# Attention of a fused transformer block: head pairs in the search for the maximum, three score banks, mask and shift through TensorE, loop written out

## The reference, cut to what matters

```
x = x + 0.5 * ffn(layernorm(x))          # x: 2 x 2048 x 256, ffn: 256 -> 1024 -> 256, then 5 spike steps
x = x + attn(layernorm(x))
x = x + 0.5 * ffn(layernorm(x))

def attn(x):                             # 16 heads of 16, causal
    q, k = rope(x Wq'), rope(x Wk'); v = x Wv' + bv
    scores = q k' / 4, future keys masked out
    return softmax(scores) v  Wo' + bo
```

## Time and profile before

| | us |
|---|---|
| median of 3 runs | 1601.37 (1593.75 to 1605.08) |
| the profiled execution: its time | 1608.4 |
| the profiled execution: its span | 1606.7 |
| mean granted clock of TensorE | 0.904 |
| busy in the span: PE / PEld / DVE / ACT / POOL | 1381.6 / 821.8 / 1139.5 / 860.6 / 229.9 |

### The profile page before, as it was taken

How to read it: one execution, slowest core, us unless ns; L and a number is a source line. 1 busy time by engine, 2 the same in 40 slices (tenths; PEclk the granted TensorE clock), 3 DMA queues, 4 the chain that set the end, 5 groups by cost and what they waited for, 6 DMA issues and landing times. The chain is left out here.

```text
span 1606.7 us, 27137 instructions
## 1 busy us (share of the span) xinstructions
PE 1381.6 (86%) x8384; PEld 821.8 (51%) x8384; DVE 1139.5 (71%) x2689; ACT 860.6 (54%) x1155; POOL 229.9 (14%) x206
## 2 busy tenths in 40 slices
PE   5988888750799999999999989999999976899997
PEld 5877777640443343343343333433433422799986
DVE  5666676821788888877887887888888930567675
ACT  5644444310036666655665665666666655466564
POOL 0012222346001011010010110110110101110100
PEclk9999999875568899997997999999999978899999
DMA  5113333437152062070080260440620002222312
GB/s 204 40 40 105 105 118 100 150 123 95 13 69 34 6 83 24 5 101 8 9 98 5 30 82 5 55 52 6 72 34 5 8 8 68 92 80 92 95 51 66
DMA packets 101898, 97.86 MB, mean 61 GB/s; under 512 B 46288, under 2 KB 85200, under 8 KB 100048
## 3 DMA queue, kind: packets, MB, share of 16 engines
q1 hardware_dynamic: 101744, 95.98, 29.0%
HBM read 57.15 MB, written 37.75 MB: 59 GB/s over the span
## 5 line engine op out<-in xcount | busy, mean ns | idle before, releaser
L1001 ACT ACTIVATE probs<-s_ps 128x1024 f32<-128x1024 f32 (+3 forms) x640 | 542.7, 895 | 327.7 <-PE s_ps L1133 326.4
L1112 PE MATMUL m_ps<-kT,qT 64*128 64x512 f32 (+3 forms) x1280 | 478.9, 478 | 112.9 <-DMA qT<-qkT_parts 55.9
L1026 DVE TENSOR_REDUCE maxes<-m_ps 128x1 f32<-128x512 f32 x768 | 490.8, 684 | 48.5 <-PE m_ps L1112 44.2
L1112 PEld LDWEIGHTS m_ps<-kT,qT 64*128 64x128 f32 x1280 | 217.2, 201 | 502.2 <-DVE maxes L1026 274.0
L1133 PE MATMUL s_ps<-qT,kT 64*128 64x512 f32 (+3 forms) x1280 | 327.3, 416 | 13.8 <-DMA qT<-shiftT 10.5
L1031 DVE CUSTOM_DVE_ANT_0 masked<-m_ps,mask_b 128x384 f32<-128x384 f32 (+3 forms) x512 | 238.3, 488 | 130.6 <-PE m_ps L1112 125.0
L1150 PE MATMUL o_ps<-probs,v_w 128*32 128x512 f32 (+3 forms) x2560 | 322.4, 578 | 0.2 <-POOL probs L974 0.2
L974 POOL TENSOR_SCALAR_AFFINE_SELECT probs<-probs 128x512 f32<-128x512 f32 x128 | 81.6, 637 | 851.8 <-ACT probs L1001 851.8
L1133 PEld LDWEIGHTS s_ps<-qT,kT 64*128 64x128 f32 x1280 | 164.2, 198 | 41.0 <-ACT probs L1001 25.0
L313 ACT ACTIVATE relu_a<-ups_a 128x512 f32<-128x512 f32 x64 | 38.1, 596 | 100.8 <-PE ups_a L562 99.9
L1150 PEld LDWEIGHTS o_ps<-probs,v_w 128*32 128x32 f32 x2560 | 51.9, 111 | 76.5 <-issue 58.9
(11 more groups left out here) (124 smaller groups left out, 1917.7 us busy)
## 6 DMA issues: line engine op xcount, KB each, us to landing
kT<-qkT_parts SPq DMA_DIRECT2D x48, 256.0 KB
qT<-qkT_parts SPq DMA_DIRECT2D x96, 128.0 KB
qkT_parts<-qk_hi_a SPq DMA_DIRECT2D x32, 256.0 KB, 3.0
qkT_parts<-qk_lo_a SPq DMA_DIRECT2D x32, 256.0 KB, 3.4
qT<-shiftT SPq DMA_DIRECT2D x512, 1.0 KB
xin_a<-in_x SPq DMA_DIRECT2D x8, 512.0 KB, 4.0
xres_a<-in_x SPq DMA_DIRECT2D x8, 512.0 KB, 4.9
x<-xsum_a SPq DMA_DIRECT2D x8, 512.0 KB, 3.2
```

Of the source, the lines that this page charges most:

```text
L1001: act.activation(probs[:, b % PBUF, 2 * hp:2 * hp + 2, off:CH], s_ps[hp][:, :, off:CH], ACT.Exp, scale=D ** -0.5)\
L1026: dve.tensor_reduce(out, m_ps[:, bank, 0:width], AX.X, ALU.max).then_inc(max_read, 1)
L1112: pe.matmul(m_ps[:, bank, 0:width], qT[of % 2][r0:r0 + HR, j, h // 2, t * P:(t + 1) * P], kT[of % 2][r0:r0 + HR, h // 2, k * CH:k * CH + w ...
```

## The change

What it does: (1) a unit of the maximum is a pair of heads, two matmuls into two banks at once; there are 80 units a group, the ring has two places of two banks, and DVE reduces both heads by one `tensor_reduce` (up to 2 x 512). (2) On the diagonal PE adds the mask by two more matmuls (bf16, identity times mask, 128 x 128), and the `tensor_tensor_reduce` goes. (3) The scores have three banks instead of four, one head each, in turn; ACT takes the exponential head by head (1280 instructions instead of 640), and PE waits for each bank by itself. (4) The two parts of the shift are turned by a transpose on PE, as an item of the ring three units behind the last unit of the step; DVE copies the 32 rows out of PSUM, and SP writes them by 4 DMAs. (5) The loop is written out; loads of the next group are spread over six slots. (6) In a slot PE's order is: scores of `hp` 0, first item, scores of `hp` 1, second item, products, the other items.

```diff
-        HR, MB = P // 2, 3
+        SB, MB = 3, 2
+        HR = P // 2
-        s_ps = [pb(f"s_ps{p}", [P, 2, CH]) for p in range(2)]
-        m_ps = pb("m_ps", [P, MB, CH])
+        s_ps = pb("s_ps", [P, SB, CH])
+        m_ps = pb("m_ps", [P, MB, 2, CH])
...
-        UNITS = [(j, t, 2 * hp + par, k, CH if k < j else P * (t + 1))
-                 for j in range(NJ) for t in range(T) for hp in range(G // 2) for k in range(j + 1) for par in range(2)]
+        UNITS = [(j, t, hp, k, CH if k < j else P * (t + 1))
+                 for j in range(NJ) for t in range(T) for hp in range(G // 2) for k in range(j + 1)]
-            cost = [u[4] + 110 for u in UNITS]
+            cost = [2 * u[4] + 110 for u in UNITS]
...
+            for n in range(GROUPS):
+                for j in range(NJ):
+                    last = max(i for i, (_, e) in enumerate(order) if e[0] == "unit" and e[1] == n and UNITS[e[2]][0] == j)
+                    after = [i for i, (_, e) in enumerate(order) if i > last and e[0] == "unit"][:3]
+                    at = after[-1] if after else last
+                    order.insert(at + 1, (order[at][0], ("shift", n, j)))
...
+                        row, c0 = HR * par + KR + a, G * T * a + G * T // 2 * par
+                        out = qT[n % 2][row:row + 1, j, :, :].rearrange("o h (t q) -> o (h t) q", t=T)
+                        sp.dma_start(out.bitcast(F32), shiftT[c0:c0 + G * T // 2, :]).then_inc(shift_in, 16)
...
+                    for h in range(G):
+                        u = G * blk + h
+                        act.wait_ge(s_done, u + 1)
+                        act.activation(probs[:, b % PBUF, h, off:CH], s_ps[:, u % SB, off:CH], ACT.Exp, scale=D ** -0.5)\
                            .then_inc(exp_done, 1)
...
+            def unit(e):                                   # DVE
+                j, t, hp, k, width = UNITS[e[2]]
+                i = ITEM[e]
+                dve.wait_ge(max_done, i + 1)
+                dve.tensor_reduce(maxes[:, j % 2, :, hp, t, k], m_ps[:, i % MB, :, 0:width], AX.X, ALU.max).then_inc(max_read, 1)
...
+            def unit(e):                                   # PE
...
+                free_bank(i)                               # wait: max_read of item i - MB
+                for par in range(2):
+                    r0 = HR * par
+                    mm = pe.matmul(m_ps[:, i % MB, par, 0:width], qT[n % 2][r0:r0 + HR, j, hp, t * P:(t + 1) * P],
+                                   kT[n % 2][r0:r0 + HR, hp, k * CH:k * CH + width], start=True, stop=True)
+                if k == j:
+                    for par in range(2):
+                        mm = pe.matmul(m_ps[:, i % MB, par, t * P:(t + 1) * P], identb[:, :], maskb[:, :],
+                                       start=False, stop=True, skip_group_check=True)
+                mm.then_inc(max_done, 1)
+
+            def turn_shift(e):
+                i = ITEM[e]
+                free_bank(i)
+                pe.wait_ge(neg_step, 3 * step_no(e[1], e[2]) + 3)
+                pe.transpose(m_ps[0:2 * G * T, i % MB, 0, 0:P], negparts[:, :, :].rearrange("p a c -> p (a c)"), ident[:, :])\
                   .then_inc(max_done, 1)
...
+                for par in range(2):                       # scores(n, j, b, hp)
+                    u = G * block_no(n, j, b) + 2 * hp + par
+                    wait(pe, exp_done, u - SB + 1)
+                    r0 = HR * par
+                    pe.matmul(s_ps[:, u % SB, off:CH], kT[n % 2][r0:r0 + HR, hp, b * P:(b + 1) * P],
+                              qT[n % 2][r0:r0 + HR, j, hp, off:CH], start=True, stop=True).then_inc(s_done, 1)
...
+            for g, (n, j, b) in enumerate(slots):
+                items = ITEMS.get(g, [])
+                scores(n, j, b, 0)
+                ring(items[:1])
+                scores(n, j, b, 1)
+                ring(items[1:2])
+                if g >= 2:
+                    products(*slots[g - 2])
+                ring(items[2:])
```

More of the change, by code:

```diff
@@ L764, in place_units @@
             return slots
[L766 to L796, removed]
+        def ring_order():
+            unit_slots, order = place_units(), []
+            for g in range(MAX_FROM, BLOCKS * GROUPS):
+                for n in range(GROUPS):
+                    order += [(g, ("unit", n, u)) for u in unit_slots.get(g - BLOCKS * n, [])]
+                order += [(g, ("sums", n, j)) for n in range(GROUPS) for j in range(NJ) if block_no(n, j + 1, SUM) == g
+                          or j == NJ - 1 and block_no(n + 1, 0, SUM) == g]
+            order.append((BLOCKS * GROUPS, ("sums", GROUPS - 1, NJ - 1)))
+            for n in range(GROUPS):
+                for j in range(NJ):
[3 more added lines that the diff above has]
+                    order.insert(at + 1, (order[at][0], ("shift", n, j)))
+            return order
@@ L798, in wait @@
+        ORDER = ring_order()
+        ITEM = {e: i for i, (_, e) in enumerate(ORDER)}
+        ITEMS = {}
+        for g, e in ORDER:
+            ITEMS.setdefault(g, []).append(e)
+        LAST_UNIT = {(e[1], UNITS[e[2]][0]): e for _, e in ORDER if e[0] == "unit"}
+        TERMS = [(m, x) for m in range(NT) for x in range(2)]
+        LOADS, SHIFTS = 16 * NT * (2 + G) + 32, 16 * 4
         def wait(eng, sem, value):
-            if not isinstance(value, int) or value > 0:
+            if value > 0:
@@ L800, in wait @@
                 eng.wait_ge(sem, value)
[L802 to L837, removed]
@@ L896, in shift @@
+                if m == 0 and x == 1:
+                    sp.dma_start(v_in[p][:, :, :], io["v"][tok:tok + S, group * G * D:(group + 1) * G * D]
+                                 .rearrange("(k p) n -> p k n", p=P)).then_inc(vs_in[p], 16)
+            def shift(n, j):
+                sp.wait_ge(max_read, ITEM["shift", n, j] + 1)
                 for a in range(2):
                     for par in range(2):
-                        row = HR * par + KR + a
-                        out = qT[dn % 2][row:row + 1, j, :, :].rearrange("o h (t r n) -> o (h t) r n", t=T, r=P // VW)
@@ new lines, in store, with moves @@
+            def store(n, j):
+                tok, group = place(n)
+                sp.wait_ge(max_read, ITEM["sums", n, j] + 1)
+                sp.dma_start(io["attn"][tok + j * CH:tok + (j + 1) * CH, group * G * D:(group + 1) * G * D]
+                             .rearrange("(t p) n -> p t n", p=P), att[:, :, :]).then_inc(att_out, 16)
+            def moves(g):
+                for what, n, j in ITEMS.get(g, []):
+                    if what == "shift":
+                        shift(n, j)
+                    elif what == "sums":
+                        store(n, j)
@@ L1010, in _ @@
+                before = (n, j)
+            read_sum(*before)
         @block.vector
         def _(dve):
[L1012 to L1033 removed]
@@ L1184, in _, with ring @@
-            pe.wait_ge(const_in, 32)
-            for x in range(MAX_FROM, 0):
-                for u in unit_slots[x]:
-                    find(0, 0, x, 0, u)
-            steps(pe, body)
+            def ring(items):
+                for e in items:
+                    if e[0] == "unit":
+                        unit(e)
+                    elif e[0] == "shift":
+                        turn_shift(e)
+                    else:
+                        turn_sums(e)
+            pe.wait_ge(mask_ok, 2)
@@ new lines, in _ @@
+            for g in range(MAX_FROM, 0):
+                ring(ITEMS.get(g, []))
+            slots = [(n, j, b) for n, j in steps() for b in range(T * j + T)]
+            for g, (n, j, b) in enumerate(slots):
[7 more added lines that the diff above has]
+                ring(items[2:])
+            for slot in slots[-2:]:
+                products(*slot)
```

369 lines of the change are left out of this document (129 added, 240 removed).

## The result

| | before | after |
|---|---|---|
| median, us | 1603.22 (1593.75 to 1606.89) | 1682.05 (1665.12 to 1688.48) |
| ratio, 95% interval | | 1.048 (1.040 to 1.056) |
| profiled execution: its time | 1608.4 | 1665.12 |
| mean granted clock | 0.904 | 0.926 |
| busy PE / DVE / ACT | 1381.6 / 1139.5 / 860.6 | 1407.4 / 1107.4 / 903.7 |

The change makes the kernel slower by 4.8%. The median moved by 79 us, the two profiled executions by 57: the one of after is its fastest, and the one of before (1608.4) lies above all four runs of its median. DVE has less to do, the clock is higher, and still it takes longer: PE's busy time grew by 26 us, and the rest is waiting.

A forecast was written before the change was run, and what follows sets the result against it. DVE and the banks it frees bound full slots; afterwards a PE-ACT chain would. At 119.4 us a group against 112.1, the main part adds 55 and the last slots 0.5 to 1608.4, about 1664; against the median 1657, range 1610 to 1720.

The forecast's parts named there:

- The chain in each slot: Main part: PE's fourth score waits for ACT's first exponential of the same slot; 2.69 us a full slot, 97.0 a group.
- ACT is not the bound, by-head exponentials cost nothing: Each full slot: four exponentials of 512 take some 2.0 us on ACT, below the chain's 2.69.
- DVE: Main part: a wide reduce takes 1.2 us, so DVE needs 88 us a group against 93 busy before.
- The mask: Diagonal units: PE's mask matmuls cost 0.4 us for each of 19 units not first in their slot, 7.6 a group.
- The clock: Main part: one full slot a group at the low clock, 4.3 us instead of 2.69, adds 1.6 us a group.
- The rest of a group: Per group: chain 97.0, unhidden pairs of item matmuls 8.4, turned sums 2.4 and turned shifts 2.4 us.
- The last 20 slots: End of the attention, without units: 14 full slots and two narrow sets take 49.5 us against 49 before.
- The turned shift: Four a group: PE waits for a reduce and three DVE operations, 0.6 us each, 2.4 a group.
- The old stall of 7.24 us: End of the kernel: scores waited for the shift's 16 DMAs; with four, taking 2.7 us, this stall goes.
- Rival 1: Main part: the chain is there but the rest hides; 106 us a group, 1555 in all; chance 0.22.
- Rival 2: Main part: the clock falls in each slot's gaps, eight more low-clock slots a group; +96 us, 1750; chance 0.12.
- Rival 3: Main part: DVE stays the bound, wide reduce 1.28 us, PE's chain fits beside it; no change, 1600; chance 0.08.

The follow-up runs named there:

- e2: Two score banks instead of three in the changed kernel; 1796.46 us, ratio 1.117 to before.
- e6: Against e3, the products cut into two halves of the queries, one behind each pair of scores; 1563.99 us, ratio 0.971 to before.
- e5: Changed kernel with whole products between the third and fourth score and the second item behind the fourth; 1670.3 us, ratio 1.031 to before.
- e8: Kernel before, each exponential of a pair made as two of one head, banks as they were; 1607.43 us, ratio 0.999 to before.
- e4: Changed kernel without the two mask matmuls of each diagonal unit; 1640.78 us, ratio 1.018 to before.
- e7: e6 without the mask matmuls; 1518.67 us, ratio 0.943 to before.
- e3: Changed kernel with the next group's loads back in pairs at slots 0, 4 and 12; 1633.11 us, ratio 1.017 to before.
- e1: Changed kernel with the whole products moved between the two pairs of scores; 1687.73 us, ratio 1.047 to before.

## Why the prediction was right, and where it wasn't

The forecast was 1657 us, slower; 1682 was measured, within its own range. (By the bounds that it names, half of -12 to +13 us a group makes 1612 to 1706; its 1720 isn't in them.) The median moved by 79 us, where 56 were forecast. By the profiled executions, on which the sum was made, it was 1664 against 1665. That is closer than the steps deserve: it sets an execution of before that is slower than all four of its median against the fastest of after, and the attention itself grew by 63 us where 55.5 were summed, which the shorter untouched parts hid.

- *The chain in each slot*: right, and shown. The full slot without units was priced at 2.69 us and takes 2.67, with two units it was to take 2.8 to 3.0 and takes 2.90. The waits turned from DVE to ACT as the prediction asked (277 us). e2 lengthened the loop by one bank fewer and e6 shortened its stretch, each slot without units to within 0.01 us of what the sum says; e5 was 0.08 shorter than its sum, by the trip.
- *ACT is not the bound, by-head exponentials cost nothing*: right, by e8.
- *DVE*: right. The wide reduce was taken at 1.2 us and has 1.225; 88 us a group were predicted, and 664.5 / 7.5 = 88.6 are there.
- *The mask*: the term was too big. 0.4 us for a unit was 0.27 to 0.31 (e4, e7), so of 7.6 us a group 5.1 to 5.9 were due. I had counted a stand ahead of the mask and part of one behind it, and the second was there without it.
- *The loads*: the step that was missing. The prediction names the part of the change that spreads them over six slots nowhere in its sum, though they stand in the same queue as the attention's store. They cost 7 us in each group that has the stall (e3), 38 us of the main part or 5.1 a group over its 7.5, and 49 us of the median. That is some 60% of the 79 by which the change is slower.
- *The clock*: 1.6 us a group were added for a low clock of unnamed place. With the loads mended the main part runs at 0.99 for 0.96, so some three quarters of its low clock came with the stall of the store. The term stood for something real, but was too small and had no cause.
- The rest of a group: 114.35 us in e3 less the mask's 5.1 to 5.9 is 108.5 to 109.2; the prediction has 97.0 + 8.4 + 2.4 + 2.4 = 110.2. The sum holds to 1 or 2 us; its single terms weren't measured.
- *The last 20 slots*: predicted 49.5, measured 57. The full slots were right. The narrow ones weren't: I took products as narrow as the slot's scores, but the products belong to the slot two earlier. Timeline of after, PE:

```profile
1350.45 0.27 PE L1007 MATMUL m_ps<-ident_b,negparts 128*32 128x128 f32 x1 [1.09 <-DVE negparts L938]
...
1353.59 0.62 PE L1026 MATMUL s_ps<-qT,kT 64*128 64x384 f32 x3
1355.04 1.06 PE L1041 MATMUL o_ps<-probs,v_w 128*32 128x512 f32 x8
1356.04 0.50 PE L1026 MATMUL s_ps<-qT,kT 64*128 64x256 f32 x3
```

The slot of 384 takes 2.45 us (1353.59 to 1356.04) where 2.24 were counted, since products of 512 stand in it; the three narrow slots end at 1360.04, so take 6.45 for 5.43. The turned shift adds a wait of 1.09 (0.6 taken), and from 1363 a stretch at the low clock follows. The old stall of 7.24 us did go: four DMAs take 2.7 us.

So errors of opposite sign met, and that is luck: per group about 2 us too much for the mask and 1 too much in the rest, against 3.5 too little for the stall (5.1 less the 1.6). The 119.4 of the sum and the 119.6 measured (897 / 7.5) agree by that. Rival 1 (the rest hides) is refuted: even with the loads mended the group takes 114.35 us, not 106, and the kernel stays 1.7% slower than before (e3). Rival 2 (the clock falls) is refuted for the change: in its full slots with gaps the clock stays high, 0.96 in the main part and 0.99 in e3. But the last slots of e1, with a gap in each, ran at 0.50 for 60 us, so what it fears does occur, and what starts it isn't shown. Rival 3 (DVE stays the bound) is refuted by its 58 us of waits.

The layout itself is the smaller part of the loss. With the loads in their old places it costs 1.7%, and with the products halved besides it is 2.9% faster than before. That this gain is DVE's smaller load is likely, but no run took the wide reduce alone, and none the written-out loop.

## What to carry to other kernels

Where an engine that works in order feeds a ring of buffers, and a step feeds it once more than it has places (here four scores on three banks), the step is at least the latency of one trip round the ring plus the longest stretch of other work between two feeds, wherever that stretch stands. Splitting it helps (e6), and so does taking something out of it (the item in e5); moving it whole doesn't (e1). The sum can be read off a few timeline rows. When a change moves loads, write down every store in the same queue and who waits for it, even if the change is about something else. A total that agrees proves no term: take the terms apart by single edits before one of them is used again.

## What the runs showed of the hardware that I had not expected

- Two short matmuls of another kind between two kinds of work cost 0.27 to 0.31 us (e4) or 0.30 (e7: 45 us over 152), where 0.22 lie between their start and the next one's. In the rows of e4 the stand is seen where the kind changes from the 64-row scores, once.
- A store of one attention tile took 11.8 us from issue to the end of DVE's wait with loads of the next group ahead of it and behind it in its queue, and PE stood for 4.67 us: the granted clock was 0.80 from 1195 to 1200, where the stand begins, and 0.52 in the next 5 us, with products of 1.94 us for 1.06.
- Before with its products halved ran at a clock of 0.82 in the main stretch, with PE busy 20.00 of 20 us in a window at 0.50; over its whole span it has 0.854, the changed kernel with the same halves 0.928, before 0.904. Nothing that I ran explains it.
